# Turning and copying a tile's rows two tiles ahead, into four buffers, in a mixture-of-experts loop

## The reference, cut to what matters

```python
def moe(x):                        # x: T = 2048 tokens by H = 256
    shared = silu(x @ sg_w.T) * (x @ su_w.T) @ sd_w.T
    scores = sigmoid(x @ gate_w.T) + gate_bias           # 64 experts in 8 groups
    ... keep the 4 best groups, then the 6 best experts, weights normed to 1
    h = silu(einsum('th,eih->eti', x, eg_w)) * einsum('th,eih->eti', x, eu_w)
    routed = einsum('eti,ehi,te->th', h, ed_w, comb)     # INTER = 128
    return shared + routed
```

## Time and profile before

| | us |
|---|---|
| median of 3 runs | 561.03 |
| lowest, highest | 559.43, 562.28 |
| the profiled execution | 560.77 |
| its span, first to last instruction | 559.0 |

### The profile page before, as it was taken

One profiled execution on the slowest core, in us unless ns is written; L12 is line 12 of the kernel. 1 busy time (PEld: TensorE's weight loads), 2 busy tenths in 40 slices (PEclk: granted clock), 3 DMA queues, 4 the chain that ended last, 5 costly groups with the idle time before them and its releaser, 6 DMA issues. The chain is left out here.

```text
span 559.0 us, 12585 instructions
## 1 busy us (share of the span) xinstructions
PE 472.0 (84%) x2990; PEld 355.2 (64%) x2991; DVE 340.1 (61%) x1054; ACT 281.2 (50%) x910; POOL 252.8 (45%) x277
## 2 busy tenths in 40 slices
PE   0466899999999999987679999999999999997923
PEld 0343676777776766654437787787787787783522
DVE  3715367998999999887753343443443444441797
ACT  2257478877788887871113444444454454441000
POOL 1100111466666666666741546555565565544000
PEclk9967689999999999997899999999999999998967
DMA  8999920011111111121234568557577746542996
GB/s 270 346 333 288 284 60 2 30 67 69 68 59 58 58 66 68 71 75 68 105 110 121 187 190 276 166 170 236 173 211 214 222 143 207 178 150 92 414 360 251
DMA packets 57589, 91.04 MB, mean 163 GB/s; under 512 B 7911, under 2 KB 44650, under 8 KB 57552
## 3 DMA queue, kind: packets, MB, share of 16 engines
q1 hardware_dynamic: 44880, 62.41, 36.9%
q0 software_dynamic: 10368, 26.07, 13.0%
q10 hardware_dynamic: 2304, 2.10, 1.1%
HBM read 87.09 MB, written 41.60 MB: 230 GB/s over the span
## 5 line engine op out<-in xcount | busy, mean ns | idle before, releaser
L392 POOL DMA_INDIRECT y_rows<-y,xring x120 | 118.0, 984 | 108.0 <-issue 67.1
L1021 PE MATMUL ps<-wring,prob 128*128 x480 | 124.5, 382 | 9.1 <-ACT prob L543 9.1
L970 DVE TENSOR_TENSOR probt<-probt,ps 128x128 f32<-128x128 f32 x120 | 34.5, 287 | 119.2 <-ACT probt L548 108.5
L1021 PEld LDWEIGHTS ps<-wring,prob 128*128 128x128 f32 x480 | 81.8, 190 | 17.6 <-issue 11.5
L450 ACT ACTIVATE prob<-ps,nmax 128x128 f32<-128x128 f32 x256 | 69.6, 388 | 5.1 <-DVE nmax L676 3.9
L1021 PE MATMUL ps<-wring,probt 128*128 x240 | 72.0, 382 | 0.0
L548 ACT ACTIVATE probt<-ps 128x128 f32<-128x128 f32 x120 | 33.3, 277 | 71.4 <-PE ps L1021 71.4
L543 ACT COPY prob<-ps 128x256 f32<-128x256 f32 x121 | 45.0, 373 | 47.4 <-PE ps L1236 44.8
L978 DVE TENSOR_SCALAR y<-ps,xring 128x256 f32<-128x256 f32 x120 | 57.8, 483 | 6.4 <-PE ps L1021 4.1
L365 POOL DMA_INDIRECT slot_rows<-row,slot_ix x48 | 52.7, 1097 | 13.7 <-issue 13.4
L365 POOL DMA_INDIRECT slot_rows<-xring,slot_ix x48 | 51.0, 1062 | 14.0 <-issue 14.0
(11 more groups left out here) (177 smaller groups left out, 779.6 us busy)
## 6 DMA issues: line engine op xcount, KB each, us to landing
wring<-wexp SPq DMA_DIRECT2D x121, 384.0 KB
xring<-slot_rows SPq DMA_DIRECT2D x121, 129.0 KB, 2.1
x_sb<-y_rows SPq DMA_DIRECT2D x16, 768.0 KB, 7.3
slot_rows<-pads SPq DMA_DIRECT2D x1, 8256.0 KB, 36.5
x_sb<-x SPq DMA_DIRECT2D x3, 2048.0 KB, 17.8
slot_rows<-pads SPq DMA_DIRECT2D x5, 516.0 KB, 10.3
x_sb<-x SPq DMA_DIRECT2D x4, 512.0 KB, 5.9
out<-h_all ACTq DMA_DIRECT2D x16, 128.0 KB, 6.9
```

Of the source, the lines that this page charges most:

```text
L392: nc.gpsimd.indirect_dma_start(out=y_dram, out_offset=bass.IndirectOffsetOnAxis(ap=xring[:, q, TO_AT:TO_AT + 1].bitcast(I32), axis=0), in_ ...
L970: nc.vector.tensor_tensor(hm[:, q % 2, :], silu[:, q % 2, :], psS[q % 2][:, INTER:2 * INTER], ALU.mult).then_inc(S("h_ready"), 1)
L1021: return nc.tensor.matmul(*a, **k)
```

## The change

Where a step handled tile t + 1, it handles tile t + `AHEAD`, with AHEAD = 2. This holds for SyncE's load, TensorE's turn and ScalarE's copy. These three engines begin at step -2 rather than -1. The copies go into four buffers instead of two (the two further ones lie in the unused halves of `prob`), and the copy waits for the up product of the tile four back. The PSUM banks of the turns stay two. The ring of weights (8), the row buffers (12) and `load_tile`'s wait on `down_done` keep their sizes and their form. At the end one dead tile more is loaded, turned and copied.

```diff
+AHEAD = 2
...
-        xt = prob[:, :, 0:KT, :]
+        xt = prob[:].rearrange("p s (h k) n -> p (s h) k n", k=KT)
...
             def load_tile(i, q, t, tail):
-                u, uq = t + 1, (q + 1) % U
+                u, uq = t + AHEAD, (q + AHEAD) % U
...
-                wait(sp, y_out[uq % NY], 16 * (U // NY * (i + (q + 1) // U - 1) + uq // NY + 1))
+                wait(sp, y_out[uq % NY], 16 * (U // NY * (i + (q + AHEAD) // U - 1) + uq // NY + 1))
                 sp.dma_start(xring[:, uq, :], slots_dram[ds(at, P), :]).then_inc(xt_in[uq], 16)
-            last = tile_loop(sp, SP, load_tile, -1, 0)
-            sp.wait_ge(xt_in[0], 16 * last + 32)
-            sp.wait_ge(w_in[0], 16 * last + 32)
+            last = tile_loop(sp, SP, load_tile, -AHEAD, 0)
+            for n in range(AHEAD):
+                sp.wait_ge(xt_in[n], 16 * last + 32)
+                sp.wait_ge(w_in[n], 16 * last + 32)
...
             def tile_step(i, q, t, tail):
-                u = t + 1
+                u = t + AHEAD
                 if not tail:
                     act.wait_ge(S("xt_done"), u + 1)
-                    wait(act, S("up_done"), u - 1)
-                    nc.scalar.copy(xt[:, (q + 1) % 2].rearrange("p a k -> p (a k)"),
-                                   psT[(q + 1) % 2][:, 0:D]).then_inc(S("xt_ready"), 1)
+                    wait(act, S("up_done"), u - 3)
+                    nc.scalar.copy(xt[:, (q + AHEAD) % 4].rearrange("p a k -> p (a k)"),
+                                   psT[(q + AHEAD) % 2][:, 0:D]).then_inc(S("xt_ready"), 1)
...
-            tile_loop(act, SCALAR, tile_step, -1, 1)
+            tile_loop(act, SCALAR, tile_step, -AHEAD, 1)
...
             def tile_step(i, q, t, tail):
-                u = t + 1
+                u = t + AHEAD
                 if not tail:
-                    uq = (q + 1) % U
-                    pe.wait_ge(xt_in[uq], 16 * (i + (q + 1) // U) + 16)
+                    uq = (q + AHEAD) % U
+                    pe.wait_ge(xt_in[uq], 16 * (i + (q + AHEAD) // U) + 16)
                     wait(pe, S("xt_ready"), u - 1)
...
-                    both(psS[q % 2][:, 0:2 * INTER], lambda k: xt[:, q % 2, k, :],
+                    both(psS[q % 2][:, 0:2 * INTER], lambda k: xt[:, q % 4, k, :],
...
-            last = tile_loop(pe, PE, tile_step, -1, 2)
+            last = tile_loop(pe, PE, tile_step, -AHEAD, 2)
             pe.wait_ge(S("y_ready"), U * last + U)
-            pe.wait_ge(S("xt_ready"), U * last + (U + 1))
+            pe.wait_ge(S("xt_ready"), U * last + (U + AHEAD))
```

## The result

| | before | after |
|---|---|---|
| median of 6 runs, us | 561.45 | 565.61 |
| lowest, highest | 556.72, 562.28 | 562.42, 567.69 |
| the profiled execution (its span) | 560.77 (559.0) | 562.42 (560.6) |

The account below looks back on a forecast made before the run. The prediction took TensorE's order of work in the tile stage as the bound. Start 0.8, first run of late loads 1.6 and five more runs 4.3 summed to +6.7 us, forecast 567.5 us, range 562.5 to 573.

Parts of the forecast that it names:

- What the change is: SyncE's load in the tile stage: issued no earlier, only its user, TensorE's turn, comes one step (1.62 us) earlier.
- Copy and buffers at 0: ScalarE's copy one step earlier into four buffers: gain 0, since no product waits for a copy.
- The start, +0.8: Start of the tile stage: third turn waits for the first copy, slot load queues behind it; +0.8 us, bounds 0.2 to 1.0.
- The first-step pauses stay: First steps of the ten passes: TensorE's 9.1 us of waits belong to the slot load and stay, about 0.9 us each.
- The waits, +5.9 (1.6 + 4.3): TensorE's earlier turns meeting unlanded row loads: 1.6 us in the first run of late loads, 4.3 in five more.
- The first run of late loads: Tiles 24 to 31: waits overlap and the largest counts, 1.9 less the 0.3 there today, so 1.6 us.
- The other five: Late loads at tiles 49, 86, 73, 56 and 97, each taken to land in 3.6 us: together 4.3 us.
- The sum: Whole kernel: 0.8 + 1.6 + 4.3 = +6.7 us, giving 567.5; ends +1.8 and +10.4.
- loads that land in time (1): Rival on row loads: late landings are chance or shift along, only the start's 0.8 is left, 561.8 us; chance 0.07.
- That delays don't add (2): Rival on SyncE's lag between runs of late loads: a delay is paid once, +2.4, 563.4 us; chance 0.12.
- That the first steps wait for the copy (3): Rival at passes' first steps: up product waits for a fresh copy, so 9.1 us go, 552.7 us; chance 0.05.
- The worse case (4): Rival: leads of about ten more tiles shrink below their landing, 0.4 us each, +4 more, 571.5 us; chance 0.14.

Follow-up runs that it names:

- e2: The kernel before with SyncE's loads held back by one tile (`down_done` >= u-6 instead of u-7), turn unchanged; ratio to before 1.0103.
- e3: The changed kernel with each tile's row load issued a step earlier, ahead of the previous tile's weights' fetch and wait on `down_done`; ratio to before 0.9975.
- e1: The kernel before with only the four buffers and the copy's looser wait; turn, copy and load stay one tile ahead; ratio to before 0.9986.
- e8: The kernel of e3 with the load of three ring slots moved ahead of the turn at each pass's first step; ratio to before 0.9972.
- e9: The kernel before with the three ring slots of a pass's first step kept in TensorE's registers instead of read from the table; ratio 0.9864, median 553.65 us.
- e6: The changed kernel with all loads held back one tile more (`down_done` >= u-6); ratio to before 1.0503.
- e7: The changed kernel with rows issued ahead of the same tile's weights' fetch, behind the same wait on `down_done`; ratio to before 1.0072.

## Why the prediction was right, and where its sizes were off

*What the change is.* Right: issues no earlier, turn one step earlier, and the lead that is lost decides. It is shown from both ends by e2 and e3.

*Copy and buffers at 0.* Right (e1).

*The start, +0.8.* Right: 2.22 - 1.39 = 0.83. The reason holds too: with the slot load first, the time is gone (e8).

*The first-step pauses stay.* Right in the cause (e9) and nearly in the size, 8.0 for 9.1. That they would keep their length was not, and the prediction had named shrinking pauses as a sign of being wrong; the cause stood all the same. The nine intervals of the up products over a pass's change sum to 24.83 us before and 24.54 after, and the latter hold two waits for rows (tiles 14 and 86). Of the other seven, five are shorter by 0.1 to 0.5, one is the same and one is 0.2 longer. Two things shrank: the product starts 0.37 us after the end of the slot load in eight of the nine, where it was 0.46 to 0.51, and the nine loads last 7.6 us in all against 8.6. The one of the step in the earlier trace rows lasts 924 ns against 1234. Why is not shown, and such loads vary.

*The waits, +5.9 (1.6 + 4.3).* **This term was too large.** From first to last up product the loop grew by 208.27 - 204.68 = 3.59 us. The first run of late loads (tiles 23 to 31) was sized well: its steps grew by 1.4 us, forecast 1.6, if the first step of the pass in its midst, whose slot load was shorter, is counted apart. The other five, forecast at 4.3, brought about 1.3: tile 49 0.3 (forecast 1.1), tile 86 0.5 (1.0), tile 73 0.1 (0.9), tile 56 0.4 (0.6), tile 97 none (0.7). There were three that I did not forecast, tiles 14, 67 and 77, together another 1.3, of which 77 alone 0.75. The sign was as announced, 6.2 us in 14 waits, but the largest single one was 0.8 us and not near 1.5. Two steps of my working failed:

1. The landings, taken at 3.6 us, were in part right (tile 49's took about 3.7), but I kept each load's *issue* where it stood. Tiles 49, 73 and 97 are the first that SyncE loads in a new pass in the kernel before, and they carry its branches. Since the loads are written for t + 2, that place is now one tile on. SyncE's issues around tile 49:

```profile
370.88 0.34 SPq L327 DMA_DIRECT2D xring<-slot_rows  x1
372.05 0.34 SPq L322 DMA_DIRECT2D wring<-wexp  x1
372.60 0.34 SPq L327 DMA_DIRECT2D xring<-slot_rows  x1
374.40 0.09 SPq L322 DMA_DIRECT2D wring<-wexp  x1
374.80 0.34 SPq L327 DMA_DIRECT2D xring<-slot_rows  x1
...
376.33 0.20 PEld L1238 LDWEIGHTS ps<-const_sb,xring 128*128 128x128 f32 x2 [0.49 <-DMA xring<-slot_rows]
```

   The long gap (2.2 us without a fetch) is now behind 372.60, the load of tile 49, so that load comes 1.7 us after the one before it. In the trace of before it came 2.45 after (373.47 to 375.92). So it waits 0.49 us. The place has moved to tiles 14 and 86, two of those that pay.
2. I measured a wait by the turn's weight load, which runs some 0.2 us ahead of its product while TensorE still multiplies. Of the 0.76 us that tile 24's weight load waits, the products see 0.36 as idle time, and the step grew by 0.64. For ten waits I estimate from this that another 1 to 2 us were too much.

The description of the kernel says that each of the 64 experts' weights is fetched once. The trace of before has 121 issues of `wring`, of which 30 take 0.34 to 0.38 us and so move weights; the others take 0.09 to 0.11. So a late load is rarer than 64 fetches in 120 tiles would make it. The sum is not touched, since it went by the issues in the trace.

*The sum.* +6.7 forecast; +4.98 in the stage (0.83 at the start, 3.59 in the loop, 0.56 behind the last up product, where the prediction had 0), +4.2 between the medians, and 5.4 by the ratio. That the total came this near is partly luck: the five forecast runs fell short by 3.0 us, and 1.3 us at tiles that I had not named and the 0.56 us of a lower granted clock made up for 1.9 of it.

The rivals: loads that land in time (1) fell by the new rows of the wait list. That delays don't add (2) was too strong: there are ten waits on weight loads, spread from tile 23 to 77, and the loop grew by 3.6 us, not by the largest. That the first steps wait for the copy (3) fell by e9. The worse case (4) did not come; e6 shows something like it one step further on. The Trainium skill's fit of a landing (page "DMA: Bandwidth & Descriptors", section "Anatomy of one DMA — SWDGE (gpsimd) path"; 2.3 us for 129 KB, an estimate from it) would have given 0.8. The trace of the changed kernel disagrees for the loads with a fetch less than 1 us ahead (2.6 to 4.2 us), and those decide.

## What to carry to other kernels

Before an operation is moved ahead, ask what it waits for and whether that moves too. A buffer that is never waited for gains nothing from a second copy, and an earlier consumer only spends the lead of its producer; here SyncE's wait was tied to tile numbers, so it stayed. A releaser that the wait list names is the last to end, not the cause: look at what the waiting engine's own queue does in that time (here a load of three table entries into registers), and test by taking that away. It was worth 1.4%, more than the change had been about: 553.65 us with kept slots and nothing else changed, faster than both kernels.

## What the runs showed of the hardware that I had not expected

Reading three words of a table into registers of TensorE's queue lasts 0.78 to 1.39 us at the passes' first steps, one word 0.30 in the median and up to 0.80 in the trace of before. Split into one and two words, the parts lasted 0.57 and 1.00 us at one of them, together more than the 1.23 of the whole load there.

A row load of 129 KB that lands in 2.2 us in the median takes up to 4.9 when weights are fetched near it (e7). A fetch ahead of it counts for most: 2.6 to 4.2 us with one less than 1 us ahead in the changed kernel, 3.2 to 4.9 with one 1.1 to 1.5 us ahead in e7, and 2.0 to 2.5 for four of the five loads in e7 that had only their own tile's fetch behind them.

The queue that issues transfers can be as tight as the engine that computes. With the pauses gone, waits for rows rose in every version with the loads of before (2.2 us in three waits in e9, where before had 0.3).
